# One crossbar transpose for both halves of the last attention's split exponentials

## The reference, cut to what matters

```python
h = jnp.maximum(_layernorm(x, axis=-1), 0.0)
# _L1_gnn_ref, NH = 8 heads of DK = 32
q, k, v = heads(x @ Wq), heads(x @ Wk), heads(x @ Wv)
scores = jnp.einsum('bhnd,bhmd->bhnm', q, k) / sqrt_dk
scores = jnp.where(mask, scores, -jnp.inf)
attn = jax.nn.softmax(scores, axis=-1)
out = jnp.einsum('bhnm,bhmd->bhnd', attn, v)     # contracts over m
x = x + jax.nn.relu(out.reshape(b, n, d)) @ Wo
```

## Time and profile before

| | us |
|---|---|
| median of 3 runs | 763.97 (763.64 to 764.99) |
| the profiled execution, its own time | 768.98 |
| its span in the trace | 767.1 |
| busy: PE, DVE, ACT, POOL | 716.1, 684.1, 592.6, 536.5 |

### The profile page before, as it was taken

How to read it: one execution, slowest core, us unless ns; L and a number is a source line. 1 busy time by engine, 2 the same in 40 slices (tenths; PEclk the granted TensorE clock), 3 DMA queues, 4 the chain that set the end, 5 groups by cost and what they waited for, 6 DMA issues and landing times.

```text
span 767.1 us, 26536 instructions
## 1 busy us (share of the span) xinstructions
PE 716.1 (93%) x8398; PEld 592.9 (77%) x8398; DVE 684.1 (89%) x2017; ACT 592.6 (77%) x1865; POOL 536.5 (70%) x733
## 2 busy tenths in 40 slices
PE   0689999999999999999999999999999999999973
PEld 0477788888878888888888888888887888888852
DVE  5878999999999999999999999999998999999772
ACT  0368888888877888887888888878887788788852
POOL 6558777777667677767777777677776767776651
PEclk9999999999999999999999999999999999999996
DMA  7123466756666565676566566665575556555574
GB/s 198 41 53 67 99 114 112 112 122 122 109 111 113 117 116 115 114 121 113 112 118 119 115 115 115 109 119 112 125 116 103 113 108 115 116 119 98 86 117 96
DMA packets 270423, 84.70 MB, mean 110 GB/s; under 512 B 242896, under 2 KB 269904, under 8 KB 270288
## 3 DMA queue, kind: packets, MB, share of 16 engines
q1 hardware_dynamic: 269856, 82.24, 58.1%
q10 hardware_dynamic: 432, 0.79, 0.5%
HBM read 15.86 MB, written 8.39 MB: 32 GB/s over the span
## 4 chain that ended last, share of the span: by engine, by line
PE 65%; DVE 13%; DMA 7%; issue 6%; SPq 4%; ACT 4%; POOL 1%; DVEq 0%; POOLq 0%; ACTq 0%
PE bank L928 24%; PE bank L954 8%; PE bank L1104 6%; PE bank L1064 5%; DMA hT<-h_split 5%; PE bank L1083 3%; PE bank L1045 3%; PE bank L1053 3%; PE bank L980 3%; DVE top L848 2%; SPq L297 2%; SPq L273 2%; ACT e L554 2%; PE bank L1006 1%; PE bank L1004 1%
## 5 line engine op out<-in xcount | busy, mean ns | idle before, releaser
L554 ACT ACTIVATE e<-bank,nmx,q_power 128x128 f32<-128x128 f32 x512 | 194.6, 480 | 5.1 <-DVE nmx L853 4.9
L408 POOL CAST e_split<-e 128x512 f16<-128x512 f32 x128 | 89.7, 701 | 116.7 <-ACT e L554 116.7
L410 POOL TENSOR_TENSOR e_split<-e,e_split 128x512 f16<-128x512 f32 x128 | 152.2, 1189 | 10.3
L954 PE MATMUL bank<-w,h1T 128*128 128x258 f32 x512 | 122.6, 381 | 0.0
L422 POOL TENSOR_TENSOR rstd<-var,minus_half 128x1 f32<-128x1 f32 x128 | 71.7, 560 | 66.4 <-DVE var L718 66.4
L928 PE MATMUL bank<-w_split,hT 128*128 128x260 f16 x768 | 98.2, 278 | 11.6 <-DMA hT<-h_split 6.3
L954 PEld LDWEIGHTS bank<-w,h1T 128*128 128x128 f32 x512 | 96.5, 190 | 15.7 <-DVE h1T L749 1.6
L505 ACT ACTIVATE eT<-lr,nmx 128x128 f32<-128x128 f32 x256 | 102.6, 456 | 0.8 <-DVE nmx L805 0.8
L928 PE MATMUL bank<-h2T,proj_split 128*128 128x128 f16 x1536 | 96.2, 219 | 1.5 <-DMA h2T<-h_split 1.5
L928 PEld LDWEIGHTS bank<-h2T,proj_split 128*128 128x128 f16 x1536 | 90.8, 98 | 3.7 <-DMA h2T<-h_split 2.1
L928 PEld LDWEIGHTS bank<-w_split,hT 128*128 128x128 f16 x768 | 71.1, 98 | 23.7 <-DMA hT<-h_split 8.3
(11 more groups left out here) (120 smaller groups left out, 1905.6 us busy)
## 6 DMA issues: line engine op xcount, KB each, us to landing
x_in<-in_x_dram SPq DMA_DIRECT2D x64, 128.0 KB, 2.4
out_dram<-x_out SPq DMA_DIRECT2D x64, 128.0 KB, 2.0
adj_in<-in_adj_dram SPq DMA_DIRECT2D x64, 64.0 KB, 2.4
e3T<-e_split SPq DMA_TRANSPOSE x128, 3.1
hT<-h_split SPq DMA_TRANSPOSE x64, 2.4
h2T<-h_split SPq DMA_TRANSPOSE x64, 2.5
attT<-att_split SPq DMA_TRANSPOSE x64, 2.7
w<-in_L_gnn_W_dram SPq DMA_DIRECT2D x2, 256.0 KB, 6.1
```

Source lines behind the costliest of these rows:

```text
L408: pool.tensor_copy(e3_split[:, g.two, half, 0], e).then_inc(s[high_set], 1)
L410: pool.tensor_tensor(e3_split[:, g.two, half, 1], e, e3_split[:, g.two, half, 0], ALU.subtract).then_inc(s[low_set], 1)
L554: ins = act.activation(e3[:, g.two, h, :], S[:, h // 4, (h % 4) * N:(h % 4 + 1) * N], ACT.Exp, bias=nmx3[:, g.two, h:h + 1], scale=q_power ...
L954: ins = pe.matmul(X2[:, 0:D + 2], h1T[:, g.two, k * F:(k + 1) * F], w2[:, k, :], start=k == 0, stop=k == H - 1)
```

## The change

The two transposes of one graph's exponentials become one of 128 x 2048, issued where the last half was issued, as the first entry of phase 9. It waits for both halves of the split. The semaphores `e3T_here` go from four to two, TensorE's `mha_av` waits for one in place of two, and GpSimd, before it overwrites a half of `e3_split`, waits for the one transpose of two graphs before.

```diff
-        e3T_here = [sem(f"e3T_here{i}") for i in range(4)]
+        e3T_here = [sem(f"e3T_here{i}") for i in range(2)]
...
-            def e3_transpose(g, half, low_set):
-                done(sp, s[low_set], g)
+            def e3_transpose(g):
+                done(sp, s["e3_low_first"], g)
+                done(sp, s["e3_low_last"], g)
                 free(sp, s["av_done"], g)
-                sp.dma_start_transpose(e3T[:, g.two, half].rearrange("p s h n -> p (s h) n"),
-                                       e3_split[:, g.two, half].rearrange("p s h n -> p (s h n)")).then_inc(e3T_here[2 * half + g.two], 16)
+                sp.dma_start_transpose(e3T[:, g.two].rearrange("p f s h n -> p (f s h) n"),
+                                       e3_split[:, g.two].rearrange("p f s h n -> p (f s h n)")).then_inc(e3T_here[g.two], 16)
...
-                (e3_transpose_last, 9), (att_transpose, 10), (store, 11), (norm1_transpose, 3), (e3_transpose_first, 8),
+                (e3_transpose, 9), (att_transpose, 10), (store, 11), (norm1_transpose, 3),
                 (load_adj, 1), (load_x, 0), (norm2_transpose, 6),
...
-                wait(pool, e3T_here[2 * half + g.two], g.dma2 - 16)
+                wait(pool, e3T_here[g.two], g.dma2 - 16)
...
                 pe.wait_ge(e3T_here[g.two], g.dma2)
-                pe.wait_ge(e3T_here[2 + g.two], g.dma2)
```

More of the change, by code:

```diff
@@ L298, in att_transpose @@
                                        att_split[:, g.two].rearrange("p s c -> p (s c)")).then_inc(attT_here[g.two], 16)
[L300 to L304, removed]
             for k in range(KD):
```

## The result

The changed kernel takes 777.21 us (median of 6 runs, 774.13 to 779.99), the kernel before beside it 763.81 (761.96 to 765.78): ratio 1.016, 95% interval 1.0141 to 1.0178. It is 13 us slower, outside the range of the forecast (763.4 to 774.0), on the side that it gave. The profiled execution has a span of 778.0 us, 10.9 more than before, and took 779.99. Both profiled executions are longer than the medians (by 2.8 us here, by 5.2 before), so the two profiles show 11 of the 13.4 us.

A forecast was written before the change was run, and what follows sets the result against it. It took TensorE's own work as the bound, `hT` close behind; 768.98 + 2.2 (disturbed steps) + 2.4 (drain) = 773.6 us profiled, scaled to a median of 768.5 us, range 763.4 to 774.0.

The forecast's parts named there:

- What bounds the kernel: Steady steps: TensorE's own work sets the 10.89 us step, with `hT` close behind, 0.75 us to spare.
- The saving is worth nothing: SP's queue: 64 issues fewer, 84 us of queue time, none of it on the path, so 0 saved.
- What the larger transpose costs SP: SP's issue of 16 blocks: 1.39 us by the slope of two measured sizes, bounds 1.26 and 2.5 us.
- The disturbed steps, +2.2 us: Steady part: steps where an instruction transfer delays `hT` make TensorE wait more, +2.2 us, bounds 0 and 4.3.
- The drain, +2.4 us: Last graphs: the whole transpose starts only where the last half's did, +1.4 and +1.0 us, bounds 1.4 and 3.5.
- `e3T` lands 4.6 us after its issue with room for `mha_av`: Steady step: the large transpose lands in 4.6 us, leaving `mha_av` 1.7 us to spare.
- Rival (b): SP's issue of 16 blocks stalls to 2.5 us, `hT` lands just when wanted: 780 us, chance 0.10.
- (a): Rival: `hT`'s spare time holds in the steady part and only the drain pays: 766.4 us, chance 0.17.
- (c): Rival: the transfer gains by size, 16 blocks taking hardly longer than 8: 764.3 us, chance 0.11.
- (d): Rival: the freed queue matters, one command fewer ending TensorE's waits for `hT`: 760.2 us, chance 0.12.
- The 261 GB/s: The skill's DMA transpose rate; with it the added 256 KB take 1.0 us, not 1.35, total 0.7 us less.
- The fetch of instructions as the disturbance: Steady part: q8 instruction transfers, one or so per step, delay `hT` when they meet `attT`, the store or `hT`.

The follow-up runs named there:

- no_first_half: The kernel before with the first half's transposes left out from graph 2 on: 764.81 us against 765.56, ratio 0.9993.
- drain_split: The changed kernel with `hT` issued directly behind the large transpose and the last four graphs transposed in two halves: 761.76 us, ratio 0.9949 to the kernel before.
- two_hT_first: The kernel before, two transposes kept, with `hT` issued directly behind the last half's, ahead of `attT` and the store: 760.60 us, ratio 0.9938.
- two_at_head: The kernel before with the first half's transpose issued in the next step, directly ahead of the last half's, unmerged: 794.81 us, ratio 1.038.

## Why the prediction was wrong, point by point

- **What bounds the kernel: right.** TensorE's own work, with `hT` 0.75 us behind it, was the right picture, and the ten kernels of the table fit it.
- **The saving is worth nothing: right.** SP's wait at `h2T` grew by 57 us and the time did not fall; no_first_half shows the same alone.
- **What the larger transpose costs SP: wrong, and the failed step.** I continued the slope of 4 and 8 blocks to an issue of 1.39 us; measured are 1.94 at the median. I let it hide in SP's wait ahead of `attT` (0.5 us), where in the step shown it did hide, and left `attT`'s own issue behind it at 1.19 us without asking. That one is stalled: 1.62 us at the median, 1.85 in the step shown. So `hT` is issued about 0.6 us later, and its spare time went from 0.75 to 0.1 us and not to the 0.6 of the forecast.
- **The disturbed steps, +2.2 us: wrong by that, and by the halving.** I had 12.5 waits of 0.84 us, 10.5 us in all. Measured are 22 of 0.58, 12.8 us; so it is their number that was short. Then I halved the increase of 4.3 us, because a TensorE that was held back would find the next `hT` early. Measured, with whatever is given back in this way already taken off, are 6.6 us more in the waits and 8.8 in the gaps; and each us of a gap is paid in full, as steady less gaps in the table shows. So the halving had no ground in the runs. And the cost is steep in the spare time, where I took it as nearly even. Spare times of 2.3, 1.4, 0.7, 0.1 and -0.6 us go with gaps of 0.2, 1.8, 5.9 to 8.8, 17.6 and 30.2 us (8.2 less the time from `h2T` to `hT` and less 2.4 us to the landing).
- **The drain, +2.4 us: right.** It is 2.2 in the profile and 2.0 to 2.2 by drain_split. The last wait for `e3T` is 4.34 us where I had 4.6, and 3.19 before.
- **`e3T` lands 4.6 us after its issue with room for `mha_av`: right.** Measured 4.8; in the steady part TensorE's only row for it is of its weight loads, 0.2 us.
- **Rival (b)** came nearest: SP's issue is stalled and `hT` comes just when it is wanted, 780 us. It put the stall into the large transpose's own issue (2.5 us), which would push `attT` back; most of what counts lies one issue later. I gave it one chance in ten because two sizes lay on a line. The profile had nothing above 8 blocks, so the slope was no evidence there, and stalled issues of up to 2.3 us were to be seen.
- **Rivals (a), (c) and (d)** fall: not the drain alone pays (the steady part has 9.8 of the 10.9 us), 16 blocks land in 4.8 us and not in 3.1, and no_first_half shows that the freed queue gives nothing.
- **The 261 GB/s** that the prediction takes from "DMA: Bandwidth & Descriptors" of the Trainium skill (Latency and other measured facts) stand there for a non-contiguous middle dimension, beside about 350 to 400 for the contiguous case. The windows here have 181 to 208 GB/s with the DMA engines full, below both.
- **The fetch of instructions as the disturbance** is supported, not tested. Before, 14 of the 15 steps with a gap have a q8 transfer that starts between 3 us ahead of `hT`'s issue and 2.2 us behind it; of the 40 steps without one, 13 do. After, it is 23 of 29, and 7 of 26. In two_hT_first such transfers fall there in 28 steps and none has a gap. An example of the kernel after, SP's timeline and the queue between 119 and 122 us:

```profile
119.24 2.56 SPq L285 DMA_TRANSPOSE hT<-h_split  x1
...
q8 instruction: 1, 0.02, 3.6%
```

Left open: what holds the issue up (the blocks that may be handed over ahead of the data, or something else), and why most issues of 16 blocks take 1.7 to 2.1 us but nine of the 64 only 1.3. No run here tells it.

## What to carry to other kernels

Ask of a merge what it moves. Joining a transfer that stood behind the tight one with one ahead of it puts both ahead; here that cost 29 us, of which the merge returned 16 to 18. Find the transfer with the least spare time (here `hT`, by landing time against its reader's start), and put everything with room behind it: one entry moved in SP's list gave 0.6%, and the merge in that same order took 3.3 us of it back. And a duration read at two sizes is not a slope to go beyond them: bound it, and give the upper bound its weight where the spare time is as small as the difference.

## What the runs showed of the hardware

- SP's issue of a crossbar transpose took 1.19 us for 4 blocks of 128 x 128, 1.26 for 8, 1.43 for 12 (one step read) and 1.94 for 16 at the median, with a transpose of 4 blocks right behind the last two stalled as well (1.62 behind 16, about 1.5 to 1.6 behind 12, 1.24 behind two of 8).
- The moving took as long per block as in smaller transposes: 2.7 us for 16 blocks and 1.35 for 8, with the DMA engines full at 208 and 190 GB/s, and the landing went from 3.1 us for 8 blocks to 4.8 for 16.
- After a gap of TensorE of 1.7 us the granted clock was 0.59 over the next 4 us once; in two_at_head it was 0.50 over a whole window of 4 us behind a longer one:

```profile
516.00:520.00 4.00, 4.00 (x35) 2.67 (x34) 2.33 (x5) 1.06 (x4) 1.05 (x2) 0.50 0.76 142
```

The length of the gap alone doesn't tell: gaps of 1.8 us in the kernel before and of 2.25 us at 113 us in two_at_head left it at 1.00. What else decides, no run here shows.
